# Decoder block on one core: the order of TensorE's work inside a tile of self- and cross-attention

## What is computed

```python
# self-attention, 16 heads of 8 channels, one bias for each head and distance
Q, K, V = (proj(Wq, bq), proj(Wk, bk), proj(Wv, bv))
scores = jnp.einsum('bhqd,bhkd->bhqk', Q, K) / math.sqrt(D_K)
scores = scores + _rel_bias_matrix(rel_bias, S)[None]
attn = jax.nn.softmax(scores, axis=-1)
out = jnp.einsum('bhqk,bhkd->bhqd', attn, V)
...
x = _layernorm(x + out @ Wo.T + bo)
# cross-attention: the queries from x, keys and values from ctx, both turned by a rotary table
q = _rope(q, T_q)
k = _rope(k, T_k)
attn = jax.nn.softmax(jnp.einsum('bhqd,bhkd->bhqk', q, k) * SCALE, axis=-1)
...
x = _layernorm(x + out @ Wo.T)
```

## Time and profile before

| What | Value |
|---|---|
| median of 3 runs | 1552.3 us (1551.49 to 1553.55) |
| the profiled execution | 1550.78 us, its span 1549.0 us |
| granted TensorE clock, mean over the span | 0.977 |
| busy: PE, DVE, ACT, POOL | 91%, 72%, 63%, 19% |
| self-attention loop in the trace | about 22 to 209 us |
| cross-attention loop | about 208 to 391 us |

### The profile page before, as it was taken

One profiled execution on the slowest core, in us unless ns is written; L12 is line 12 of the kernel. 1 busy time (PEld: TensorE's weight loads), 2 busy tenths in 40 slices (PEclk: granted clock), 3 DMA queues, 4 the chain that ended last, 5 costly groups with the idle time before them and its releaser, 6 DMA issues. The chain is left out here.

```text
span 1549.0 us, 32429 instructions
## 1 busy us (share of the span) xinstructions
PE 1410.6 (91%) x12666; PEld 864.9 (56%) x12666; DVE 1112.9 (72%) x2348; ACT 979.0 (63%) x1524; POOL 297.6 (19%) x274
## 2 busy tenths in 40 slices
PE   6999999998899799898998878999999999999984
PEld 4666666666566344343443354666666666666652
DVE  4666778886433899999999954355667776776688
ACT  2233367676555899999999954455555665665546
POOL 3433244452001011110110031111111221220000
PEclk9999999999899999999999999999999999999996
DMA  5000000000100000000000002222222222222210
GB/s 185 3 2 2 2 15 16 13 9 3 55 1 1 1 2 1 1 1 1 1 1 4 1 14 59 70 64 64 64 62 62 62 62 62 62 62 62 69 42 21
DMA packets 40246, 49.74 MB, mean 32 GB/s; under 512 B 8992, under 2 KB 22944, under 8 KB 39712
## 3 DMA queue, kind: packets, MB, share of 16 engines
q1 hardware_dynamic: 39808, 47.01, 11.8%
q10 hardware_dynamic: 288, 0.67, 0.2%
HBM read 13.04 MB, written 2.10 MB: 10 GB/s over the span
## 5 line engine op out<-in xcount | busy, mean ns | idle before, releaser
L2065 DVE TENSOR_TENSOR l_px<-psum,l_share 128x1024 f32<-128x1024 f32 x64 | 78.4, 1225 | 152.3 <-PE psum L1572 102.1
L1810 ACT ACTIVATE l_prob<-psum,l_bias 128x1024 f32<-128x1024 f32 x64 | 71.4, 1115 | 174.1 <-PE psum L1543 174.1
L1555 PE MATMUL psum<-l_XT,l_A 128*128 128x256 f32 x512 | 125.3, 389 | 1.1 <-ACT l_XT L1828 1.1
L1538 PE MATMUL psum<-l_th,l_XT 128*128 128x512 f32 x256 | 124.1, 607 | 1.6 <-DVE stream L2072 0.8
L1572 PE MATMUL psum<-l_prob,l_X 128*128 128x512 f32 x256 | 121.3, 596 | 0.7 <-DVE l_px L2065 0.7
L1618 PE MATMUL psum<-l_px,l_N 128*128 128x256 f32 x480 | 115.0, 383 | 0.0
L2042 DVE TENSOR_REDUCE l_top<-psum 128x8 bf16<-128x1024 f32 x64 | 78.2, 1221 | 36.6 <-PE psum L1635 36.6
L1555 PEld LDWEIGHTS psum<-l_XT,l_A 128*128 128x128 f32 x512 | 93.5, 192 | 11.9 <-ACT l_XT L1828 1.4
L1277 DVE TENSOR_TENSOR f_frac<-f_whole,psum 128x1024 f32<-128x1024 f32 x80 | 97.7, 1221 | 2.7
L1273 DVE TENSOR_SCALAR f_whole<-psum 128x1024 f32<-128x1024 f32 x80 | 97.4, 1218 | 1.6 <-PE psum L894 1.6
L1618 PEld LDWEIGHTS psum<-l_px,l_N 128*128 128x128 f32 x480 | 87.6, 190 | 16.1 <-issue 5.0
(11 more groups left out here) (355 smaller groups left out, 3243.8 us busy)
## 6 DMA issues: line engine op xcount, KB each, us to landing
l_share<-l_recip SPq DMA_DIRECT2D x496, 64.0 KB, 2.0
early_weights<-in_weights SPq DMA_DIRECT2D x1, 2405.0 KB, 11.2
c_cs<-in_ctx SPq DMA_DIRECT2D x16, 128.0 KB, 2.1
f_qf<-in_l_mats SPq DMA_DIRECT2D x1, 2048.0 KB, 7.8
out<-l_normed SPq DMA_DIRECT2D x16, 128.0 KB, 2.0
l_craw<-in_ctx SPq DMA_DIRECT2D x15, 128.0 KB, 2.3
late_weights<-in_weights SPq DMA_DIRECT2D x1, 1089.0 KB, 11.2
relbias<-in_relbias ACTq DMA_DIRECT2D x1, 512.0 KB, 5.1
```

The source lines that it names most:

```text
L1538: nc.tensor.matmul(ps[:, SC + n, :], XT[:, q % 3, k, :, :], th[:, q % 2, k, 8 * n:8 * n + 8, :], start=True, stop=False)
L1555: last = nc.tensor.matmul(ps[:, at + j // 2, (j % 2) * 256:(j % 2 + 1) * 256], A[:, QB * k + j, :], XT[:, q % 3, :, 1, :], start=True, sto ...
L1810: nc.scalar.activation(prob[:, b % 4, :, :], ps[:, SC:SC + 2, :], ACT.Exp, bias=bias[:, b:b + 1]).then_inc(s["exped"], 1)
L2065: nc.vector.tensor_tensor(px[:, q % 2, :, k, :], ps[:, at:at + 2, :].rearrange("p a (h s) -> p (a h) s", s=S), share[:, (b // 2) % 2, b % ...
```

## The change

In the loop of self-attention, `a_scores(n + 2)` now stands in front of `turn_out(n - 1)`, and `project_out(n - 1)` behind the duo's input projection. In the loop of cross-attention, `columns_of(d)` stands behind `turn_out`. No instruction is added or removed; only TensorE's list changes, those of the other engines are the same.

```diff
                         columns_of(d - D)
+                if n + 2 < NT:
+                    a_scores(n + 2)
                 if n >= 1:
                     turn_out(n - 1, a, A)
-                if n + 2 < NT:
-                    a_scores(n + 2)
                 if n == NT - 2:
                     rough(0)
...
-                if n >= 1:
-                    project_out(n - 1, a, A, "a_wo")
                 if n % 2 == 0:
                     if d < D:
                         a_project_in(d)
                     else:
                         project_in(d - D)
+                if n >= 1:
+                    project_out(n - 1, a, A, "a_wo")
                 weigh(n, a, A)
...
                 scores(n)
-                if n % 2 == 0 and d < D:
-                    columns_of(d)
                 if n >= 1:
                     turn_out(n - 1, s, C)
                 else:
                     turn_out(NT - 1, a, A)
+                if n % 2 == 0 and d < D:
+                    columns_of(d)
```

## The result

| | before | after |
|---|---|---|
| median of the runs | 1552.9 us | 1542.6 us |
| the profiled execution | 1550.8 us, span 1549.0 | 1543.3 us, span 1541.4 |
| ratio after / before | | 0.9936, 95% interval 0.9921 to 0.9951 |

One of the six runs of the kernel before took 2010.6 us, far outside the others, and stands in the median of the table but not in the ratio; the five others have a median of 1552.3 us. By the ratio the kernel is faster by 9.9 us, and the interval is 7.6 to 12.3 us. The forecast was 1543.0, 9.3 us faster.

The account below looks back on a forecast made before the run. TensorE was taken to bound the self-attention loop. The terms -5.5 - 1.3 - 3.0 + 0.5 = -9.3 us from the profiled 1550.8 give 1541.5, and 1.5 us for the median gives 1543.0 us, range 1540.0 to 1548.5.

Parts of the forecast that it names:

- The bound and the cause: Self-attention loop: TensorE busy 179.70 of 187 us; 5.5 us idle before L291, of which 5.4 wait for VectorE's a_ao.
- The even tiles, -5.5 us: Self-attention, even tiles 4 to 24: the wait at L291 goes, 0.50 us in each of eleven tiles.
- the upper bound of 0.56: Even tiles of self-attention: at most 0.56 us saved per tile, if TensorE's pipeline refilling also goes; 6.2 us in all.
- L165 as the tightest point: Even tiles of self-attention: L165, now before L297, needs a_xT and has a margin of 0.06 us.
- Tile 25, -1.3 us: Self-attention tile 25: L291's wait shrinks from 1.68 to 0.46 us, saving 1.3 us; bounds 0 and 1.7.
- The clock behind tile 25, -3.0 us: Self-attention after tile 25: with the shorter gap no clock fall is expected, saving 3.0 us; bounds 0 and 3.0.
- The first tile of cross-attention, +0.5 us: There the four turnings begin only behind L291, costing 0.5 us; the gap grows from 0.99 to 1.6 us.
- rival (1): The clock fall moves to the new 1.6 us gap in cross-attention's first tile, costing 3.0 us: 1546.0 us; chance 0.19.
- a fall of the clock at a new place: Sign against the prediction, which expected the clock to be full from 160 to 200 us.
- The other even tiles of cross-attention, 0: L291 moves ahead of the turnings by 0.5 us at no cost, covered by ScalarE's exponent; uncovered, 2.8 us over 14 tiles.
- The range: Whole kernel: 1540.0 to 1548.5 us, from the forecast's own bounds 1540.8 and 1545.3 and low-bound rivals reaching 1548.3.
- (2): The clock fall stays at or near tile 25, having another cause than this gap: 1546.0 us; chance 0.17.

Follow-up runs that it names:

- e6: Kernel before with VectorE's moments of the residual moved behind the division in the next even tile, TensorE's order untouched: 1545.0 us against 1552.0, ratio 0.9951.
- e2: Kernel before with only the output projection moved behind the input projection in self-attention: 1551.3 us against 1552.7, ratio 0.9994.
- e1: Kernel before with only the scores moved in front of the turning of outputs in self-attention: 1551.0 us against 1552.7, ratio 0.9989.
- e3: Kernel before with only the columns moved behind the turning of outputs in cross-attention: 1553.7 us against 1552.7, ratio 1.0006.
- r1: Kernel before profiled again, nothing changed: self-attention loop 183.8 us, tile 25 7.11 us, no fall of the clock.
- r3: Full change profiled again, nothing changed: loop 174.9 us, first tile of cross-attention 7.73 us, no fall of the clock.

## Why the prediction was right, point by point

- **The bound and the cause.** Right. TensorE bounds self-attention, and the loss in even tiles was VectorE's lateness with a_ao; e6 removes it from VectorE's side and gets 5.5 us in the loop without touching TensorE's order.
- **The even tiles, -5.5 us.** Right in mechanism, too small in size: -6.6 us in tiles 4 to 24, and tiles 26 and 2 and those from 27 on, which the prediction left out, give 0.6, 0.2 and 0.3 more. 0.60 a tile is above the upper bound of 0.56. Tile 2, from which I took the cost of a tile without a wait, has one: L185 to L297 is 1.14 us there too. I had used its first step only, and did not see that the wait in front of L291 covers a second one in front of L297, which the new order takes away as well (e6, and tile 2 in e2). The 0.06 us that the upper bound adds says nothing sure of a wait: the record of L291 is 0.33 us in the profile after too, where it waits for nothing.
- **L165 as the tightest point.** Right, no wait in any even tile; the margin is 0.05 us in the profile after, reckoned as there, against 0.06 worked out.
- **Both moves are needed.** The prediction gave this no sentence. Each alone gives nothing in the even tiles from 4 to 24 (5.99 and 5.97 us, e1 and e2), both give 0.6.
- **Tile 25, -1.3 us.** 1.1 us (7.11 to 6.02). From start to start L291 comes 0.66 us later than without a wait (the record says 0.60), and not 0.46: TensorE is there 0.10 us earlier, since tile 24 is 0.60 us shorter and not 0.50, and a_ao comes 0.09 later, since L185 begins 0.37 us behind L158 and not 0.28.
- **The clock behind tile 25, -3.0 us.** Right between the two first profiles, wrong as a term of the median. The fall costs 2.6 us net (9.69 to 7.11), as the slow L199 at its end lay over a wait that tile 26 would have had. It comes only in some executions: two of the five profiles with the 1.68 us gap. So it is worth about 1 us in the mean. This is the step that failed: one fall in one profile was taken as the gap's price each time.
- **The first tile of cross-attention, +0.5 us.** +0.27 us (e3), and rival (1) with it in two of the four profiles with the longer gap, +1.5 and +1.6 us (9.21 and 9.35 against 7.73), half of its price of 3.0. The prediction named a fall of the clock at a new place as a sign that it was wrong. The profile after has that sign, so by its own test its account of the clock failed, while the total held.
- **The other even tiles of cross-attention, 0.** Right to 0.01 us in the starts of tiles 1 to 30; the moved step stands in thirteen of them, not 14.
- **The range.** Its lower end was added up wrongly: with 6.2 and 1.7 us the forecast's own bound is 1541.9, not 1540.8. The upper one, 1545.3, is right.
- **The sum.** With what the traces show at a steady clock: 6.6 + 0.6 + 0.2 + 0.3 + 1.1 - 0.3 = 8.5 us (the loops of r1 and r3, both without a fall, differ by 8.8, and the first tile of cross-attention takes 0.3 of it back), and the two clock terms in the mean 2.6 x 2/5 - 1.5 x 2/4 = 0.3, so 8.8 us. The measured 9.9 us hold this in their interval (7.6 to 12.3). That the forecast of 9.3 was so close is luck: a tile term 2 us too small and a clock term 2 us too large nearly cancel.

In the two first profiles rival (1) is what happened: one gap and its fall went, and another gap of nearly that length came with a fall. Over all profiles neither rival holds as it was put. The fall comes in some executions alone, which is against (1); it came in these two places only behind the long gap, which is against (2). What decides in which execution it comes was not found. The 1 us or so between 8.8 and the measured 9.9 is inside the interval and needs no cause. The Trainium skill (TensorE: Matmul & The Clock Gate, the part on HAM oscillation) names idle gaps longer than any of these as what brings the clock down; four of ten gaps of 1.56 to 1.68 us had a fall behind them here, so these traces don't agree that only the longer ones do.

## What to carry to other kernels

When two waits on one engine follow each other, the later hides behind the earlier; price a removed wait by a tile that has neither, or take it away from the other side by an experiment, before bounding the gain. Put independent work between a step and the consumer of its result at every link of the chain (here division, turning, copy, projection): filling one link alone only moves the wait to the next. A term that rests on one fall of the clock in one profile is a chance, not a saving.

## What was not expected of the hardware

TensorE's clock fell behind a gap of 1.56 to 1.68 us in the midst of dense work in four of ten cases (tile 25: two of six, of which one has a gap of 1.56; first tile of cross-attention: two of four), and in none of the eighteen cases of these two places where the gap was 1.0 us or less, in fourteen profiles. The lower clock, 1.2 GHz, lasted 6.8 us in the former place and 3.4 us in the latter (by the granted clock), and cost 2.6 us and 1.5 to 1.6 us. The same program in the same order fell in one execution and not in the next.

The length of one gap is not all of it. In tile 30 of self-attention L248 stood still for 1.13 to 1.47 us in all fourteen profiles, and no fall followed. At the end of cross-attention, where L297 of the last tiles waited 1.0 us, the clock fell in all fourteen, though no gap of TensorE between the first tile of cross-attention and that place was longer than 1.02 us. What the two places differ in for the clock was not tested.
